# Last layer's products in another order, a copy and a PSUM slot moved, and products that nobody reads in two waits

## The reference

```python
# layer 0: attention with 8 heads of 32
qkv = (tokens @ w_proj + b_proj).reshape(B, N, 8, 96); q, k, v = split(qkv)
attn = softmax(einsum('bihd,bjhd->bijh', q, k) * 32**-0.5, axis=2)
x = einsum('bijh,bjhd->bihd', attn, v).reshape(B, N, 256) @ w_out + b_out + tokens
# layer 1: attention of one head behind a group norm (32 groups of 8 channels, over the image)
hn = (xg - mean) * rsqrt(var + 1e-6) * gn_w + gn_b
x = x + wo @ (softmax(q @ k.T / 16) @ v) + bo          # q, k, v from hn
# layer 2: the same with a norm for each channel; q and k from norm(x), v from x
# layer 3: kt, and from a 3x3 mean of x (16 x 16) qt and vt; a softmax within windows of 16
# channels, two mixtures weighted by pi; w_out; then a norm over all images, and + x
out = conv1x1(einsum('bnk,bkd->bnd', (softmax(kt2) @ vt2 * pi).sum(1) / sqrt(32), qt), w_out)
out = (out - out.mean((0, 2, 3))) * rsqrt(out.var((0, 2, 3)) + 1e-5) * bn_w + bn_b + x
```

## Time and profile before

| | before |
|---|---|
| median of three runs | 2946.13 us (2945.25 to 2949.44) |
| profiled execution | 2946.01 us, its span 2944.3 us |
| granted TensorE clock, mean | 0.949 |
| busy share of the span | PE 90%, PEld 63%, DVE 67%, ACT 44%, POOL 24% |
| chain that ended last | PE 80%, DVE 8%, ACT 5%, issue 5%, SP's queue 1% |

### The profile page before, as it was taken

The page is one execution under the profiler, slowest core; times in us unless marked ns, Lnnn a source line. Parts: engine busy times, 40 slices in busy tenths (PEclk is TensorE's granted clock), DMA queues, the critical chain, the costliest instruction groups (busy, mean ns, idle before and its releaser), DMA issues.

```text
span 2944.3 us, 43959 instructions
## 1 busy us (share of the span) xinstructions
PE 2645.1 (90%) x15676; PEld 1842.3 (63%) x15676; DVE 1984.8 (67%) x2297; ACT 1288.2 (44%) x1874; POOL 705.4 (24%) x444
## 2 busy tenths in 40 slices
PE   5999999899898998989989899898998899898994
PEld 4447765477655775557755677456774477655772
DVE  2766677666875767666776677765777666876666
ACT  3453335533364433644346333463335533365333
POOL 0530035300371013600236002440035300362011
PEclk7899999999999998999999999899999999999997
DMA  4200041000500005000050002300032000500016
GB/s 125 65 15 1 12 100 37 16 1 11 136 1 16 1 11 136 2 16 1 29 119 1 16 12 56 81 2 15 12 76 61 16 1 12 119 18 1 1 44 281
DMA packets 46237, 123.51 MB, mean 42 GB/s; under 512 B 9904, under 2 KB 21424, under 8 KB 42416
## 3 DMA queue, kind: packets, MB, share of 16 engines
q1 hardware_dynamic: 46000, 120.36, 15.2%
HBM read 41.96 MB, written 23.86 MB: 22 GB/s over the span
## 4 chain that ended last, share of the span: by engine, by line
PE 80%; DVE 8%; ACT 5%; issue 5%; SPq 1%; DMA 0%; DVEq 0%; ACTq 0%
PE tile L1520 25%; PE pv L1520 11%; PE pv L1643 8%; PE tile L1605 8%; PE tile L1633 6%; PE tile L1766 4%; PE tile L1667 4%; PE pv L1633 2%; DVE small L1112 2%; PE pv L1896 2%; PE tile L1788 2%; PE tile L1817 2%; PE tile L1695 1%; PE tile L1678 1%; ACT p L845 1%
## 5 line engine op out<-in xcount | busy, mean ns | idle before, releaser
L1112 DVE TENSOR_REDUCE small<-tile 128x1 f32<-128x1024 f32 x512 | 600.8, 1216 | 174.9 <-PE tile L1605 174.7
L845 ACT ACTIVATE p<-tile 128x512 f32<-128x512 f32 (+1 forms) x632 | 405.5, 690 | 238.6 <-PE tile L1633 236.9
L1605 PE MATMUL tile<-stack 96*128 96x512 f32 x1024 | 370.9, 461 | 43.9 <-DVE small L1112 17.1
L736 POOL TENSOR_TENSOR row_sum<-act 128x256 f32<-128x256 f32 x32 | 41.6, 1318 | 1521.3 <-DVE act L1305 1521.3
L1520 PE MATMUL tile<-qk_r 128*128 128x512 f32 x1536 | 378.0, 395 | 0.0
L706 POOL TENSOR_TENSOR acc<-acc,p 128x1024 f32<-128x1024 f32 x144 | 339.5, 2388 | 0.6 <-ACT p L845 0.6
L1520 PEld LDWEIGHTS tile<-qk_r 128*128 128x128 f32 x1536 | 287.4, 188 | 66.4 <-issue 7.7
L1605 PEld LDWEIGHTS tile<-stack 96*128 96x128 f32 x1024 | 187.3, 204 | 225.0 <-issue 114.9
L1310 DVE TENSOR_TENSOR pl<-p,ph 128x1024 fp32r<-128x1024 f32 x128 | 158.2, 1236 | 221.0 <-ACT p L925 221.0
L1633 PE MATMUL tile<-stack 112*128 112x512 f32 x760 | 270.2, 424 | 14.7 <-DVE rec L1160 8.1
L1643 PE MATMUL pv<-p,v 128*32 128x512 f32 x2048 | 272.7, 606 | 1.4 <-ACT p L845 1.4
(11 more groups left out here) (282 smaller groups left out, 4450.5 us busy)
## 6 DMA issues: line engine op xcount, KB each, us to landing
stack<-qk_r SPq DMA_DIRECT2D x192, 256.0 KB, 5.1
x_in<-in_x_dram SPq DMA_DIRECT2D x8, 1024.0 KB, 5.0
act<-in_x_dram SPq DMA_DIRECT2D x8, 1024.0 KB, 4.9
x_scratch<-act SPq DMA_DIRECT2D x7, 1024.0 KB, 4.0
z_scratch<-act SPq DMA_DIRECT2D x7, 1024.0 KB, 6.5
stack<-ones SPq DMA_DIRECT2D x16, 256.0 KB, 5.9
w3f<-w3f_scratch SPq DMA_DIRECT2D x8, 512.0 KB, 3.2
fin_rest<-z_scratch SPq DMA_DIRECT2D x3, 1024.0 KB, 9.9
```

The source lines that it names most:

```text
L845: sc.activation(p0[:, jt % DEPTH, pair, first:first + len(heads) * HALF], tile_wait(batch, "st0", *u, jt, k), ACT.Exp, scale=float(D) ** - ...
L1112: ve.tensor_reduce(maxima[:, h * NT + it:h * NT + it + 1], t, X, ALU.max).then_inc(vector_done, vector.one("max0", g, h, it))
L1605: ins = mm(o[:, s], stack[0:IMAX, g, 0, h, it * P:(it + 1) * P], stack[0:IMAX, g, 1, h, s], start=True, stop=True)
```

## The change

- **Norm of layer 1.** A helper `warm(bank, n)` issues n products 128x512 of loaded weights into an unused part of a tile. Twelve stand ahead of the first three products of the norm, five between these and the fourth, eight behind it.
- **First row maxima.** Ahead of `m0` of the first unit PE waits for ACT's second eviction of z and then issues nine such products.
- **Last layer.** `qk0(0, 1)` and `qk0(1, 1)` are cut in two halves. The first half of `qk0(0, 1)` stays ahead of the scores, the second comes with score tile 2; `qk0(1, 1)` goes from tile 2 to tiles 10 and 11. mt goes to tile 1, smt to 4 and 5, z in halves to 7, 9, 12, 14. On DVE five operations (`mixed_weights`) go from ahead of the first row maximum to behind it, `mixing` goes one tile on, and the four `z_stat` go from among the maxima to key tiles 2 to 5 of unit (0,0). ACT's evictions of smt and of the first half of z now stand ahead of those of `qk0(1, 1)`. SP issues the ones ahead of the second twelve when `qk0(1, 1)` is done.
- **Copy.** ACT's eviction of the second v0 tile goes ahead of all of layer 2's q and k, that of the first behind all of them.
- **Slot.** The last unit's tiles begin in slot 0, not 2.

```diff
@@ scalar_steps
         s += [("std", layer)] + [("norm_hi", layer, k, ct) for k in range(2) for ct in range(CT)]
+        s += [("v0_kept", 1)] if layer == 2 else []
...
-                s += [("qk_hi", layer, t, ct)] + ([("v0_kept", ct)] if (layer, t) == (2, 0) else [])
+                s += [("qk_hi", layer, t, ct)]
+        s += [("v0_kept", 0)] if layer == 2 else []
...
-    s += [("mix_exp",), ("g_kept", 0), ("g_kept", 1), ("qk0_hi", 1, 1), ("qk0_full", 1)]
-    s += [("smt_kept", 0), ("smt_kept", 1), ("z_kept", 0), ("z_kept", 1)]
+    s += [("mix_exp",), ("g_kept", 0), ("g_kept", 1), ("smt_kept", 0), ("smt_kept", 1)]
+    s += [("z_kept", 0), ("qk0_hi", 1, 1), ("qk0_full", 1), ("z_kept", 1)]
@@ PSUM slots
+        if n == ("st0", *UNITS[-1], 0, 0):
+            rings[ring] = 0
@@ SP
-                if first:
-                    sp.wait_ge(tensor_done, tensor.at(n, "qk0", 1, 1))
-                else:
-                    sp.wait_ge(tensor_done, tensor.at(batch, "smt", 1))
+                sp.wait_ge(tensor_done, tensor.at(n, "qk0", 1, 1))
                 key_ones(1)
@@ DVE
                 for k in range(G * HT):
-                    if body and k == 2:
+                    if body and k == 1:
+                        mixed_weights()
+                    if body and k == 3:
                         mixing()
-                    if body and k in (10, 13):
-                        z_stat((k - 10) // 3)
...
+                        if body and not former and jt in range(2, 2 + 2 * CT):
+                            z_stat(*divmod(jt - 2, 2))
@@ PE
+                def warm(bank, n):
+                    for _ in range(n):
+                        mm(bank, w0h[:, 0, 0, 0:P], w0h[:, 1].rearrange("p s c -> p (s c)")[:, 0:HALF], start=True, stop=True)
...
+                        o = free("gn")
+                        warm(o[:, HALF:N], 12)
                         vector_wait("mv", 1, 1)
-                        o = free("gn")
                         mm(o[:, 0:2], gn_avg[:], mv[:, :, 0], start=True, stop=True)
                         mm(o[:, 2:4], gn_rest[:], mv[:, :, 0], start=True, stop=True)
                         mm(o[:, 4:6], gn_avg[:], mv[:, :, 1], start=True, stop=False
                            ).then_inc(tensor_done, tensor.one("gn"))
+                        warm(o[:, HALF:N], 5)
                         vector_wait("gn")
                         mm(o[:, 4:6], gn_avg[:], gsq, start=False, stop=True
                            ).then_inc(tensor_done, tensor.one("pv_groups"))
+                        warm(o[:, HALF:N], 8)
...
                 if head:
-                    qk0(0, 1)
-                if body:
-                    mt_tile()
+                    qk0(0, 1, (0,))
                 for k in range(G * HT):
+                    if body and k == 1:
+                        mt_tile()
+                    if head and k == 2:
+                        qk0(0, 1, (1,))
                     if body and k == 2:
                         g_tile()
-                    if head and k == 2:
-                        qk0(1, 1)
-                    if body and k in (2, 4):
-                        smt_tile(k // 2 - 1)
-                    if body and k in (6, 9):
-                        z_tile(k // 3 - 2)
+                    if body and k in (4, 5):
+                        smt_tile(k - 4)
+                    if body and k in (7, 9, 12, 14):
+                        z_half(*((0, 0), (0, 1), (1, 0), (1, 1))[(7, 9, 12, 14).index(k)])
+                    if head and k in (10, 11):
+                        qk0(1, 1, (k - 10,))
                     if head:
                         s0(*rows_of(UNITS[0], k))
                 if head:
+                    if body:
+                        scalar_wait("z_kept", 1)
+                        warm(pv[:, 0:HALF], 9)
                     m0(*UNITS[0])
```

More of the change, by code:

```diff
@@ L119, in tensor_steps @@
         s += [("den", layer, 1), ("pv", layer, NT - 1)]
[L120 removed]
+    s += [("kt", 0), ("qk0", 0, 0), ("qk0", 1, 0), ("kt", 1), ("qv",)]
     for k in range(G * HT):
[L122 removed]
+        s += {1: [("mt",)], 2: [("qk0", 0, 1), ("g",)], 4: [("smt", 0)], 5: [("smt", 1)], 9: [("z", 0)], 11: [("qk0", 1, 1)],
+              14: [("z", 1)]}.get(k, [])
         s += [("s0", *rows_of(UNITS[0], k))]
@@ L219, in vector_steps @@
                 s += [("add0", *u, jt - 1, pair)] if jt and adder(*u, jt - 1, pair) == "vector" else []
+            s += [("z_stat", *divmod(jt - 2, 2))] if not last and jt in range(2, 2 + 2 * CT) else []
         if following:
@@ L878, in turn @@
                                           ).then_inc(scalar_done, scalar.one("norm_hi", layer, k, ct))
+                    if layer == 2 and not last:
+                        v0_kept(1)
                     for t in range(2):
@@ L883, in turn @@
                                           ).then_inc(scalar_done, scalar.one("qk_hi", layer, t, ct))
-                            if (layer, t) == (2, 0) and not last:
-                                v0_kept(ct)
+                    if layer == 2 and not last:
+                        v0_kept(0)
                     def v_hi(l, k):
@@ L1441, in turn @@
                     max_rows(*UNITS[0])
+                else:
+                    for ct in range(CT):
+                        z_stat(ct, 0)
+                        z_stat(ct, 1)
                 batch = b + 1
@@ L1590, in turn, with qk0 @@
                 kts = range(CT)
-                def qk0(t, g):
-                    o = free("qk0", t, g)
-                    for s in halves:
+                def qk0(t, g, parts=(0, 1)):
+                    o = free("qk0", t, g) if 0 in parts else where("qk0", t, g)
+                    for s in (halves[k] for k in parts):
                         ins = three(o[:, s], [[w[:, kt_, t, g * P:(g + 1) * P] for kt_ in kts] for w in (w0h, w0l)],
                                     [[x0[:, part, kt_, s] for kt_ in kts] for part in range(2)])
-                    ins.then_inc(tensor_done, tensor.one("qk0", t, g))
+                    if 1 in parts:
+                        ins.then_inc(tensor_done, tensor.one("qk0", t, g))
                 def s0(g, h, it):
@@ L1888, in smt_tile, with z_half @@
                     ins.then_inc(tensor_done, tensor.one("smt", ct))
-                def z_tile(ct):
-                    o = free("z", ct)
+                def z_half(ct, k):
+                    o = where("z", ct) if k else free("z", ct)
                     for kt_ in kts:
-                        if ct == 0:
+                        if (ct, k) == (0, 0):
                             scalar_wait("smt_kept", kt_)
-                        for s in halves:
-                            ins = mm(o[:, s], g_pi[:, kt_, ct * P:(ct + 1) * P], smt[:, kt_, s],
-                                     start=kt_ == 0, stop=kt_ == CT - 1)
-                    ins.then_inc(tensor_done, tensor.one("z", ct))
+                        ins = mm(o[:, halves[k]], g_pi[:, kt_, ct * P:(ct + 1) * P], smt[:, kt_, halves[k]],
+                                 start=kt_ == 0, stop=kt_ == CT - 1)
+                    if k:
+                        ins.then_inc(tensor_done, tensor.one("z", ct))
                 head, body = not last, not first
```

30 lines of the change are left out of this document (15 added, 15 removed).

## The result

The changed kernel took 2959.48 us (median of 11 runs, 2954.07 to 2967.90) against 2945.84 (11 runs, 2943.43 to 2949.44): a ratio of 1.0049, interval 1.0042 to 1.0057. It is slower by half a per cent, 22 us above the forecast. The profiled execution took 2960.28 us.

A forecast was written before the change was run, and what follows sets the result against it. The prediction took TensorE to bound the kernel (90% busy, 80% of the chain). Against the profiled 2946.0, -14.8 - 8.1 + 12.0 - 3.8 + 2.8 + 3.0 = -8.9 gave 2937 us, range 2914 to 2960.

The forecast's parts named there:

- copy: At layer 2's k products, PE's wait for ACT's second v0 eviction goes: 14.8 us, seven times 2.1.
- slot: At the last unit's first tile, the wait for the reciprocal that frees a slot goes: all 8.1 us.
- norm at the jumps: At layer 1's norm, products behind the jump delay q, partly repaid by its faster clock: +2.0 a jump, six jumps, +12.
- norm without a jump: In the first and last pass the twelve products lie in a wait and the clock holds: -3.8 together.
- last layer: Maxima done 5.1 earlier, but exponents wait for late transfers and PE restarts at half clock: +0.4 a pass, seven passes, +2.8.
- first image: In the first image the transfers land at 103 to 106, its third key tile having begun at 102.36: +3, once.
- Its slot is free after nine maxima: ... = 783.5: In the last layer, the reckoned time when `qk0(1, 1)` gets its slot, starting the estimates to the transfers' landing at 809.1.
- The second gap: At the norm, a 0.9 us gap in PE's instruction stream some fifteen instructions behind the jump, falling amid the twelve products.
- a rival with a chance of 24%: At the norm, the clock stays low until q runs: +4.8 a jump instead of 2.0, total 2954; chance 24%.
- The rival that the products hold the clock: At the norm, products hold the clock or lose nothing: 2929 with +0.7 a jump, 2914 with -1.9; chance 14%.
- the transfers take longer: In the last layer, the second group's transfers take 19.1 or more: +2 to +4 in seven passes, 2951 to 2965; chance 8%.
- the three signs: Prediction wrong if exponents don't wait for DMA, q starts at half clock, or products begin while the jump should still run.

The follow-up runs named there:

- copy_slot: The kernel before the change with only the copy and slot edits added; 2922.10 us, ratio 0.9924.
- last_back: The changed kernel with the last layer's order, statistics, ACT order and SP's wait as before; 2926.45 us, ratio 0.9942.
- qk_early: The changed kernel with `qk0(1, 1)` at score tiles 6 and 7, not 10 and 11, its evictions ahead of z's; 2898.51 us, ratio 0.9844.
- qk_no_nine: The changed kernel with `qk0(1, 1)` at tiles 6 and 7, its evictions ahead of z's, without the nine products before the turning; 2927.10 us, ratio 0.9935.
- norm_back: The changed kernel without the twelve, five and eight products at the norm; 2940.03 us, ratio 0.9989.

## Why the prediction was wrong

Its terms against the stretches (before to after, in us over the run; the profiled times differ by 14.3):

| term | predicted | measured | how |
|---|---|---|---|
| copy | -14.8 | -17.3 | 7 x 2.47 in its stretch |
| slot | -8.1 | -9.6 | 1.2 in seven passes and in the first image |
| norm at the jumps | +12.0 | +13.2 | 6 x (4.1 - 1.9) |
| norm without a jump | -3.8 | -2.7 | 1.4 and 1.3 |
| last layer | +2.8 | +28.8 | 7 x (6.0 - 1.75 - 0.14) |
| first image | +3.0 | +5.2 | to the second turning |
| last pass, the rest | 0 | -3.1 | not foreseen; the other traces scatter by 7 there |
| sum | -8.9 | +14.5 | |

The step that failed is "Its slot is free after nine maxima: ... = 783.5", and with it the term of the last layer, which was off by 26 us: the whole error and a little more. The mechanism was the right one (the tile late, the transfers late, the exponents waiting at the third key tile, a pause, a restart at half clock); its size was not. Counted from the first issue, the first half of `qk0(1, 1)` was to start at 22.6 and started at 25.9 (787.88 - 762.00). Behind it every step took what I had given it: PE, ACT and POOL 8.1 until the issue at 34.0 (I had 8.3), the transfers 17.3 until the third key tile at 51.3 (I had 17.3 too). So 3.3 us that were missing ahead of the ninth maximum went through whole, and a gain of 1.8 at the third key tile became a loss of 1.4.

What I had missed there is in DVE's timeline of the changed kernel:

```profile
769.06 1.22 DVE L1118 TENSOR_REDUCE small<-tile 128x1 f32<-128x1024 f32 x1 [1.45 <-PE tile L1619]
...
775.69 0.15 DVE L1426 COPY pairs<-pv 128x4 f32<-128x4 f32 x1
775.87 1.39 DVE L1428 TENSOR_TENSOR pairs<-pairs 128x2 f32<-128x2 f32 x1
...
778.29 2.35 DVE L1118 TENSOR_REDUCE small<-tile 128x1 f32<-128x1024 f32 x2
781.56 2.35 DVE L1118 TENSOR_REDUCE small<-tile 128x1 f32<-128x1024 f32 x2 [0.91 <-PE tile L1619]
785.44 2.36 DVE L1118 TENSOR_REDUCE small<-tile 128x1 f32<-128x1024 f32 x2 [1.53 <-PE tile L1619]
```

and in POOL's:

```profile
774.88 2.37 POOL L681 TENSOR_TENSOR qk_r<-qk_full,qk_r 128x1024 fp32r<-128x1024 f32 x1 [6.33 <-ACT qk_full L820]
```

Three things make up the 3.3. The first tile had to wait for the first group's landing (the 1.19 of PE's row), since only half of `qk0(0, 1)` covers it now: its maximum began 7.1 after the first issue, not 6.6. The mixing took 2.6, from 775.69 to 778.29, and not 1.5, because its second operation took 1.39: it ends at 777.26, with POOL's low part of `qk0(0, 1)` at 777.25. This operation of two columns over the whole run (duration ns min/median/max) takes 0.16 only where no head runs beside it:

```profile
L1428 DVE TENSOR_TENSOR pairs<-pairs x8: 161/1408/1462, 421.0 to 2916.0; 128x2 f32<-128x2 f32 x8
```

The Trainium skill (GPSIMD Engine Reference, Specifications) says that GpSimd shares its way to SBUF with VectorE, to the harm of operations with two SBUF inputs; this one has two, and the rows agree. And DVE idled 2.4 instead of my 0.7, because smt waited for the slot of a maximum (2.83 at 779.57), PE paused, the clock fell and the next z products ran at half of it (0.66 in the window from 780): maxima late, smt late, clock low, maxima later. I had put the low clock only behind the wait for the transfers. Counted from the first issue the maxima were so turned only 1.7 sooner here (799.65 - 762.00 against 800.33 - 760.95), where I had 5.1; but it is the transfers that count.

The restart behind the wait cost 1.8 by the same counting (19.0 from the third key tile to the second turning before, 20.8 after), where I had a net of 2.2. In other passes the stretch grew more, to 35.7.

The rest stood in the main. Copy and slot brought what their waits showed, with nothing behind them (copy_slot). The norm came out near its forecast, 2.2 a jump where I had 2.0, but by errors that cancel, and that is luck. The second gap came where it was put, behind the sixth product; the twelve ended 7.2 to 8.5 after the last product instead of 8.6; q's stretch gave back 1.9 and not 2.6. In half of the jumps the clock was back among the twelve, a little sooner than forecast, and the net is +1.1. In the other half it fell among the first six and came back only just ahead of q, which I had only as a rival with a chance of 24%; the net there is +3.3 and not the rival's +4.8, since q came 5.2 later and not 6.0, and itself started at full clock. I had read the clock at one jump. In four of the six jumps of the kernel before it was still full while the norm's first products ran and fell only behind them, as at the next jump (windows as above):

```profile
1284.00:1285.00 1.00, 0.83 (x6) 0.74 (x6) 0.00 (x0) 0.00 (x0) 0.00 (x0) 1.00 0.08 16
1285.00:1287.00 2.00, 0.00 (x0) 0.00 (x0) 0.32 (x2) 0.00 (x0) 0.00 (x0) 0.74 0.00 0
```

The rival that the products hold the clock came true in no jump of the changed kernel. It isn't ruled out by the jump standing ahead of them, as I had argued: in last_back the clock held from the pass's last product to q in three of the six jumps (q 12.7 after that product, 2.5 later than before, less the 1.9 that q's stretch gives back: near this rival's +0.7), and in qk_early in two. The first jump of last_back:

```profile
564.50:577.00 12.50, 7.08 (x33) 5.51 (x33) 5.99 (x20) 2.90 (x4) 0.00 (x0) 1.00 0.02 5
```

The advice of the Trainium skill (TensorE: Matmul & The Clock Gate, Why this matters for your kernels) to leave no idle gaps agrees with the nine products ahead of the turning, which hold it (29 us between qk_early and qk_no_nine, half of it there).

The measured time lies in the range of the rival "the transfers take longer" (2951 to 2965), but not for its reason: they took what the forecast had given them (13.81 to issue, 17.3 to the third key tile); they went out later. The bound of +2 a pass was too narrow for the +4.1 that came: once the exponents wait for the transfers, each microsecond of delay ahead of the issue is a microsecond of the pass, seven times over, and 2 us was little for a chain of eight estimates. None of the three signs that were to show the prediction wrong came: the wait was there, q started at full clock, the products began behind the jump. None of them looked at a size; the sign that did, a first turning about 5 us sooner, failed with 1.7.

Open is why norm_back gained some 1.6 a pass in the last layer, and what decides in which jumps the clock falls early, late or not at all.

## What to carry to other kernels

When a producer is moved later to even out an engine's work, follow its tile through every engine and queue to the last transfer's landing, and to who waits for that; a buffer that shares memory with the source of a transfer has a hidden reader. Here 12 transfers of 17 us needed their tile four steps sooner, and the same change with it there is 1.6% faster than before instead of 0.5% slower. Products that keep a clock up must lie wholly in a wait: behind a jump they stand in the instruction stream's own gaps, and what is put ahead of waiting work delays it. And read the clock at every pass: of six jumps here, four differed from the one that I had read.

## What the runs showed of the hardware

- A jump back on PE took 3.3 to 4.0 us in the traces of all these kernels, and a second gap follows behind six products in the new block, whether they are of 512 columns or of 2; it ends 5.4 to 6.7 us after the last product of the pass. In the kernel before the same gap stands behind the norm's first three products of two parts each, six as well.
- The spread of runs grew from 6 us in the kernel before to 14 in the changed one. In one execution the six jumps differ by up to 3 us, as the clock falls before the unread products or among the first six of them.
- An operation of DVE on two columns took 1.4 us instead of 0.16, and ended with the POOL operation of two tensors that ran beside it, within 0.02 us in all seven passes.
- A kernel whose clock is higher (0.960 against 0.949) was slower: the mean granted clock alone does not tell which kernel is faster.
